# First dense product of the graph layer computed with its result already turned; weight scales from norms; late partial rows kept in SBUF

## What is computed

```
def gcn_conv(x, W, b, src, dst, n_nodes):
    h = x @ W
    deg = segment_sum(ones, dst); dinv = rsqrt(deg)
    msgs = h[src] * (dinv[src] * dinv[dst])[:, None]
    return segment_sum(msgs, dst) + b

# x + gcn_conv(relu(gcn_conv(layernorm(x), W1, b1)), W2, b2), then
xn = l2norm(layernorm(x)); logits = xn @ (scale * l2norm(phi))   # 32 x 32 slots
d_w, c_w = softmax(logits, over slots of an expert), softmax(logits, over all)
slots = einsum('bld,bles->besd', xn, d_w)
eo = gelu(slots @ w1 + b1) @ w2 + b2
return x + einsum('bkd,blk->bld', eo, c_w)
```

## Time and profile before

| | us |
|---|---|
| median of 3 runs | 3336.66 |
| lowest and highest | 3330.42 and 3339.79 |
| the profiled execution, own time | 3334.27 |
| its span in the trace | 3332.5 |
| PE busy in it | 3109.9 (93%) |
| DVE busy | 1899.1 (57%) |
| POOL busy | 1894.5 (57%) |
| ACT busy | 1152.4 (35%) |
| TensorE clock granted, mean | 0.975 of full |

### The profile page before, as it was taken

How to read it: one execution, slowest core, us unless ns; L and a number is a source line. 1 busy time by engine, 2 the same in 40 slices (tenths; PEclk the granted TensorE clock), 3 DMA queues, 4 the chain that set the end, 5 groups by cost and what they waited for, 6 DMA issues and landing times. The chain is left out here.

```text
span 3332.5 us, 55557 instructions
## 1 busy us (share of the span) xinstructions
PE 3109.9 (93%) x18917; PEld 1984.9 (60%) x18917; DVE 1899.1 (57%) x3045; ACT 1152.4 (35%) x1379; POOL 1894.5 (57%) x1804
## 2 busy tenths in 40 slices
PE   3769999999999999889999999999999998689998
PEld 1336766667676767555666666666666653345665
DVE  7864444444444444357777777777777773101332
ACT  4832332232322222234444444444444441111000
POOL 3377777777777777377666666666666631100000
PEclk8979999999999999899999999999999999889999
DMA  8789999999999999499989888999998879999995
GB/s 308 273 322 352 322 332 323 328 330 323 334 324 331 321 334 323 160 338 353 310 310 315 305 308 305 309 312 308 310 310 311 304 251 348 320 325 267 269 274 166
DMA packets 341258, 1021.87 MB, mean 307 GB/s; under 512 B 146808, under 2 KB 150162, under 8 KB 332016
## 3 DMA queue, kind: packets, MB, share of 16 engines
q0 software_dynamic: 137376, 664.09, 57.3%
q1 hardware_dynamic: 189416, 314.66, 29.1%
q10 hardware_dynamic: 14200, 39.58, 3.7%
HBM read 876.65 MB, written 135.08 MB: 304 GB/s over the span
## 5 line engine op out<-in xcount | busy, mean ns | idle before, releaser
L1570 POOL DMA_INDIRECT xs<-table,idx x833 | 873.4, 1049 | 481.7 <-PE m_part L1747 281.8
L1051 POOL DMA_INDIRECT xs<-table,idx x833 | 927.4, 1113 | 301.1 <-issue 186.4
L1747 PE MATMUL m_part<-xs 128*128 128x512 f16 (+1 forms) x3332 | 587.8, 329 | 27.9 <-DMA xs<-table,idx 22.0
L1321 PE MATMUL a_part<-xs 128*128 128x512 f16 (+1 forms) x3332 | 583.6, 329 | 30.5 <-DMA xs<-table,idx 19.6
L1303 PE MATMUL a_ps_o<-Ws,xs 128*128 128x512 f16 (+1 forms) x3456 | 577.6, 326 | 0.0
L1747 PEld LDWEIGHTS m_part<-xs 128*128 128x128 f16 x3332 | 418.6, 142 | 167.0 <-issue 47.1
L1321 PEld LDWEIGHTS a_part<-xs 128*128 128x128 f16 x3332 | 414.5, 142 | 159.9 <-issue 41.7
L1303 PEld LDWEIGHTS a_ps_o<-Ws,xs 128*128 128x128 f16 x3456 | 338.1, 98 | 219.3
L1776 PE MATMUL m_ps_l<-xs,m_xT 128*128 128x512 f16 x1764 | 388.7, 379 | 1.4 <-issue 1.3
L1763 PE MATMUL m_ps_s<-dw_mem,xn_mem 128*128 128x512 f16 x1296 | 311.3, 380 | 2.8 <-DVE xs L1637 2.8
L1776 PEld LDWEIGHTS m_ps_l<-xs,m_xT 128*128 128x128 f16 x1764 | 172.3, 98 | 208.8 <-issue 3.1
(11 more groups left out here) (413 smaller groups left out, 3700.5 us busy)
## 6 DMA issues: line engine op xcount, KB each, us to landing
xs<-in_L_ffn_w_dram SPq DMA_DIRECT2D x64, 1152.0 KB, 10.4
xs<-table SPq DMA_DIRECT2D x98, 384.0 KB, 6.2
xs<-table,idx POOLq DMA_INDIRECT x1666, 5.6
cw_dram<-xs SPq DMA_DIRECT2D x49, 512.0 KB
table<-arena SPq DMA_DIRECT2D x49, 384.0 KB, 3.7
table<-xs SPq DMA_DIRECT2D x49, 384.0 KB
xs<-x_pad SPq DMA_DIRECT2D x49, 384.0 KB, 5.9
x_dram<-xs SPq DMA_DIRECT2D x49, 384.0 KB, 5.6
```

What stands on the lines that cost most here:

```text
L1051: pool.indirect_dma_start(out=ring[:, t, :], out_offset=None, in_=table, in_offset=bass.IndirectOffsetOnAxis(ap=idx[:, k:k + 1], axis=0)). ...
L1321: mm = nc.tensor.matmul(part[:, bass.ds(to + a, z - a)], pick[:, i % 2, :, t], ring[:, n % RING, half * D + a:half * D + z], start=False, ...
L1570: pool.indirect_dma_start(out=ring[:, t, :], out_offset=None, in_=table, in_offset=bass.IndirectOffsetOnAxis(ap=idx[:, n:n + 1], axis=0)). ...
L1747: mm = nc.tensor.matmul(part[:, bass.ds(off + at, e - f)], pick[:, i % 2, :, t], ring[:, n % RING, half * D + f:half * D + e], start=False ...
```

## The change

1. The first dense product is computed with its roles exchanged: pieces of W1 (128x128) are the stationary operand, the turned rows `vT` move, 128 columns at a time. The result comes out turned, [feature, node], in six units of 128 features with 18 matmuls each (`hidden`), 108 in all in place of 36, laid into free columns of `ps_o` and `ps_t` (`unit_place`). The second turn on PE (12 transposes), its two copies, the bias step and the 768-wide ReLU and split are gone. For each unit DVE reads it, adds the bias per partition and multiplies by a factor per node (`hidden_read`), ACT takes the ReLU as the high half (`hidden_high`), and DVE writes the low half (`hidden_low`): 12 DVE and 6 ACT instructions of 128 columns for each bin.
2. The factor per node now lies along the free axis. It is turned once (one transpose), written to a DRAM tensor `fac_dram`, and SP loads for each bin one row of it, 512 bytes, to all partitions (`fac`).
3. The second product follows its bin by two iterations instead of three; PE's tail has one bin less, and the store follows by three instead of four.
4. The scales of the weights come from the square sum (ACT, `accum_out`, with a ones matmul across partitions and a root) in place of the largest magnitude; the preparation of the weights is put in another order.
5. In `mixture`, the results of units 16 to 30 are kept in SBUF, in places where the expert weights of the last groups have been (`kept`), and DVE adds them from there. 15 of the 31 stores to `part_dram` and 15 of its loads are gone.

```diff
+        def unit_place(m, c):
+            if m == last:
+                both = part[:, 0:P], part[:, 512:512 + P], part[:, 1024:1024 + P], part[:, 1536:1536 + P]
+            else:
+                both = (ps_o[:, D:D + P], ps_o[:, D + P:D + 2 * P]) * 2
+            return (*both[0:2], ps_s[:, 512 - P:512], ps_s[:, 1024 - P:1024], *both[2:4])[c]
+
+        def units_whole(m, c):
+            return DC * m + c + 1 + (m < last and c in (0, 4))
...
+                    m = i - 1
+                    if 0 <= m < NBR:
+                        of_m = own_block(sp, tab, m)
+                        wait(sp, h_read, DC * (m - 1))
+                        sp.dma_start(fac[:, m % 2, :], fac_dram[bass.ds(of_m, 1), :].to_broadcast([P, P])).then_inc(fac_in[m % 2], 16)
...
-                    j = i - 4
+                    j = i - 3
...
+                def hidden_high(i, c):
+                    k = DC * i + c
+                    act.wait_ge(h_read, k + 1)
+                    wait(act, prod2, i)
+                    nc.scalar.activation(hT[:, 0, c * P:(c + 1) * P], t_h[:, c, :], ACT.Relu).then_inc(ht_hi, 1)
...
-                    link(v.tensor_copy(wm[:, :], ps_o[:, 512:514]))
-                    link(v.scalar_tensor_tensor(bm[:, :], wm[:, 0:1], float(D), bm[:, :], ALU.mult, ALU.add))
+                def first_scale():
+                    v.wait_ge(f1_sum, 1)
+                    v.tensor_copy(fsum[:, 0:1], ps_s[:, 0:1]).then_inc(f1_read, 1)
+                    v.wait_ge(normed1, 1)
+                    link(v.tensor_scalar(bm[:, :], wm[:, 0:1], float(D) ** 0.5, None, ALU.mult))
...
-                weight_maxima()
                 choose(1)
+                first_scale()
...
                 add_own_rows(0)
+                first_low()
                 column_sums()
+                second_scale()
...
+                def hidden_read(i, c):
+                    v.wait_ge(prod1, units_whole(i, c))
+                    if c == 0:
+                        v.wait_ge(fac_in[i % 2], 16 * (i // 2 + 1))
+                        wait(v, ht_lo, DC * i)
+                    v.scalar_tensor_tensor(t_h[:, c, :], unit_place(i, c), bcol[:, c:c + 1], fac[:, i % 2, :], ALU.add, ALU.mult).then_inc(h_read, 1)
+
+                def hidden_low(i, c):
+                    v.wait_ge(ht_hi, DC * i + c + 1)
+                    wait(v, prod2, i)
+                    v.scalar_tensor_tensor(hT[:, 1, c * P:(c + 1) * P], t_h[:, c, :], 0.0, hT[:, 0, c * P:(c + 1) * P],
+                                           ALU.max, ALU.subtract).then_inc(ht_lo, 1)
...
+                def hidden(m, first, end):
+                    for c in range(first, end):
+                        if c == 4 and m < last:
+                            pe.wait_ge(h_read, DC * m + 2)
+                        for d in range(DC):
+                            for half, Wp in ((0, W1s[0]), (0, W1s[1]), (1, W1s[0])):
+                                mm = nc.tensor.matmul(unit_place(m, c), Wp[:, d, c * P:(c + 1) * P], vT[:, half, d * P:(d + 1) * P],
+                                                      start=(d == 0 and half == 0 and Wp is W1s[0]), stop=(d == DC - 1 and half == 1))
+                        mm.then_inc(prod1, 1)
...
-                    if i >= 3:
-                        pe.wait_ge(ht_hi, i - 2)
-                        pe.wait_ge(ht_lo, i - 2)
-                        pe.wait_ge(biased, i - 1)
-                        if i == 3:
-                            pe.wait_ge(lo2, DC)
+                    if i >= 2:
+                        second_waits(i - 2)
                         product(hT, W2s).then_inc(prod2, 1)
...
-                    if i >= 2:
-                        pe.wait_ge(h_lo, i - 1)
-                        pe.wait_ge(vt_hi, i)
-                        pe.wait_ge(vt_lo, i)
-                        turn(h2).then_inc(h_turned, 1)
...
-                        product(vT, W1s).then_inc(prod1, 1)
-                    steps(10, CT)
+                        wait(pe, t_lo, i - 1)
+                        hidden(i - 1, 0, 2)
+                    steps(9, 10)
+                    if i >= 1:
+                        hidden(i - 1, 2, 4)
+                    steps(10, 11)
+                    if i >= 1:
+                        hidden(i - 1, 4, DC)
+                    steps(11, CT)
...
+                        if k >= KEPT:
+                            act.wait_ge(up, NG - 1)
+                            if k >= KEPT + G * DC * H // D:
+                                act.wait_ge(down, NG)
+                            nc.scalar.activation(kept[k], ps_o[:, k % 2, 0:D], ACT.Copy, scale=inv[:, 0:1]).then_inc(act_done, 1)
+                            continue
```

More of the change, by code:

```diff
@@ L1018, in _ @@
             def _(sp):
-                for i in range(NBR + 4):
+                for i in range(NBR + 3):
                     if i < NBR:
@@ L1090, in t_high @@
                         wait(act, stored[j % 2], 16 * (j // 2))
[L1091 to L1093 removed]
+                        nc.scalar.activation(stage[:, j % 2, 0:D], ps_o[:, 0:D], ACT.Copy, scale=out2[:, 0:1]).then_inc(t_hi, 1)
+                def hidden_high(i, c):
[3 more added lines that the diff above has]
+                    nc.scalar.activation(hT[:, 0, c * P:(c + 1) * P], t_h[:, c, :], ACT.Relu).then_inc(ht_hi, 1)
+                for i in range(NBR + 1):
                     if i < NBR:
@@ L1311, in turn, with turn_v, hidden_waits, second_waits @@
                     return mm
+                def turn_v(m):
+                    pe.wait_ge(v_lo, m + 1)
+                    wait(pe, vt_hi, m)
+                    wait(pe, vt_lo, m)
+                    if m == 0:
+                        pe.wait_ge(f1_read, 1)
+                    if m == NORM_AT - 1:
+                        pe.wait_ge(rooted, 1)
+                    turn(v2).then_inc(v_turned, 1)
+                def hidden_waits(m):
+                    pe.wait_ge(vt_hi, m + 1)
+                    pe.wait_ge(vt_lo, m + 1)
+                    wait(pe, h_read, DC * m)
+                def hidden(m, first, end):
+                    for c in range(first, end):
+                        if c == 4 and m < last:
[5 more added lines that the diff above has]
+                        mm.then_inc(prod1, 1)
+                def second_waits(m):
+                    pe.wait_ge(ht_hi, DC * (m + 1))
+                    pe.wait_ge(ht_lo, DC * (m + 1))
+                    wait(pe, t_lo, m)
+                    if m == 0:
+                        pe.wait_ge(lo2, DC)
                 for i in range(NBR):
@@ L1844, in mixture @@
         assert LOW_AT < EARLY
+        KEPT = next(k for k, g in up_at.items() if g == NG - 2)
+        KEPT_DOWN = next(k for k, g in down_at.items() if g == NG - 1)
         w1s = (w1_first, w1_second)
```

244 lines of the change are left out of this document (110 added, 134 removed).

## The result

| | before | after |
|---|---|---|
| median, us | 3335.87 (3330.42 to 3339.79, 4 runs) | 3303.10 (3298.73 to 3308.97, 4 runs) |
| profiled execution, us | 3334.27 | 3298.73 |
| its span, granted clock | 3332.5, 0.975 | 3297.0, 0.979 |

The ratio is 0.9903, with a 95% interval of 0.9887 to 0.992: 32.8 us less by the medians, 35.5 us less from one profiled execution to the other. The forecast was 3296 us, 41 us less. Two further comparisons of the same kernel gave 3304.4 (0.9905) and 3304.1 us (0.990). The profiled execution was the fastest of its four, 4.4 us under their median, where the forecast had allowed 2.4.

A forecast was written before the change was run, and what follows sets the result against it. PE was taken to bound the steady bins, with gathers and wipes pacing the start. Terms 25.3 + 4.8 + 5.9 + 5 = 41.0 us off 3334.27 give 3293.3, as median 3296 us; forecast 3286 to 3303 (0.64), 8 in 10 from 3284 to 3320.

The forecast's parts named there:

- The steady bins: First layer: a bin falls from 24.11 to 23.56 us on PE, 25.3 us over 46 iterations.
- the tail: End of the first layer on PE: 20.3 us instead of 26.2, a gain of 5.9 us, bounds 4 and 7.
- the start: First bins of the first layer: bin 3 starts near 253.5 us instead of 258.34, 4.8 us gained, ends 0 and 8.
- a to e: Steady bins: turned-row copies, unit 4's wait for DVE, DVE's load, the last low half and SP's factor load stay hidden.
- (f), POOL: Steady bins: gathers nearly fill 24.1 us, read as slack; low halves taken as zero cost, +0.3 us a bin as rival.
- The rival of the weight loads: Steady bins: weight loads don't hide in long runs; a bin 4.05 us longer at 0.098, whole 3507 us; chance 0.10.
- the last unit's chain: Tail of the first layer: the last unit's chain, which nothing hides, adds 1.4 us.
- The mixture: Mixture: fewer stores shorten PE's waits for expert weights, 5 us gained, ends 0 and 10.
- the two waits named: Mixture: PE's waits for expert weights of 5.91 and 4.36 us; fewer stores can take the second off.

The follow-up runs named there:

- runs of 36 and 108: Changed kernel with the 108 short matmuls of a bin in one run instead of three of 36 with 4 long ones between: 3299.95 us, ratio 0.9894.
- fourteen: All profiled executions whose mixture was compared: four without kept rows took 559.2 us there on average, ten with them 552.6.
- the late load: Changed kernel with the 3 MB load of phi, and the squares made from it, four bins later in the first layer: 3300.05 us, ratio 0.9901.
- the changed kernel's second profile: The changed kernel itself, unedited, run again as the measure on the same chip: 3304.42 us, ratio 0.9905.

## Why the prediction was right, and where it was off

The measured median, 3303.10 us, lies in the range of 8 in 10, at the very edge of the forecast's own bracket (3286 to 3303). Its largest term was right in its mechanism and somewhat too large, the tail was right, and the start failed. The 35.5 us between the two profiled executions flatter the forecast: by the medians it is 32.8, and 0.9 of the 35.5 lie in the second layer, which the change doesn't touch.

**The steady bins: mechanism right, size 25.3 forecast, 21.9 measured.** The bin was to be 23.56 us and is 23.62, and before it was 24.10 in nearly all bins, not the 24.11 of the one that was read. (Each kernel has one bin that is 1.7 us longer, with four matmuls for the sum of phi's squares in it.) The largest part is the mis-sized short matmul: 0.0554 us taken from runs of 12, 0.0558 in runs of 36 and 108, so 6.03 and not 5.98 us for the product, 2.3 us over 46 bins; the other 0.02 us a bin are as small as the reading of a row. All that had to stay hidden stayed hidden (a to e): the line of the short matmuls shows 1.5 us of waits in the whole layer, none for DVE. (f), POOL: no wait for tiles in a steady bin, the six low halves hold a gather for nothing that shows, and the stretched gathers shrank (1.13 us busy for one in the earlier trace rows, 1.03 after). That reading, slack taken up, was right, but the slack was only 0.55 us a bin more than what was used.

**The rival of the weight loads is refuted** by the runs of 36 and of 108, both at 55.8 ns. The rule of the Trainium skill (TensorE: Matmul & The Clock Gate, section Back-to-back issue gap) of about 81 ns for a pair of 128 columns differs from this; the measurement decides. By the same section an isolated gap is 128/2.4 + 2.5 = 55.8 ns, and that is what the stream of fresh loads ran at here.

**The start: 4.8 forecast, 0.4 measured, the step that failed.** The prediction took bin 2's last gather at 245.96 and 5 to 6 us of landing for the end of that bin. In the changed kernel the wait for the wipe, the two turns and the product were out of the way as forecast, and then the gathers stood in their place: the median gather issued between 230 and 260 us took 11.7 us to land (6.2 in the steady bins), since 3 MB of phi fill the DMA engines there. The trace of before has the same stretch, in its busy time by stretch:

```profile
240.00:260.00 20.00, 18.52 (x122) 12.82 (x121) 7.44 (x10) 3.40 (x4) 15.43 (x16) 0.98 1.02 404
```

The prediction read a stretch from 166 to 250 us instead, in which this is averaged away to 0.88. It also put bin 3's start down to the wipes and the turns alone, though PE waited for gathered rows in that bin before the change too:

```profile
244.56 0.87 PE L1321 MATMUL a_part<-xs 128*128 128x512 f16 x4 [0.91 <-DMA xs<-table,idx]
245.91 0.86 PE L1321 MATMUL a_part<-xs 128*128 128x512 f16 x4 [0.49 <-DMA xs<-table,idx]
```

The load is in both kernels and costs both some 4 us there. So the 4.8 us compared a bin 3 without it (253.5) with one that had it (258.34), and booked the load's price as the change's gain. A second part: the prediction had DVE reach bin 0's sums some 2 us earlier, but its preparation now lies on bin 0's gathers and ends that bin some 2.6 us later (27.4 against 30.0 us from the same gather). From bin 0's end to bin 3 the changed kernel needs 50.7 us with the load out of the way and the kernel before 52.9 to 53.7; with the load in place it is 52.8 to 54.9 us in four executions, for 56.7 and 58.5. So the change gives 2 to 4 us behind bin 0, and pays about as much in bin 0.

**The tail: 5.9 forecast, 5.8 measured**, with 20.4 for 20.3 us; the last unit's chain shows as 1.16 us.

**The mixture: 5 forecast, 6.3 in the pair of profiles, 6.6 over fourteen.** The later of the two waits named (4.36 us) went, with its burst at the lower clock (5.73 to 4.08 us). That the earlier one shrinks is not shown. (One figure of the prediction is off: 322 GB/s over 24.1 us are 7.8 MB, not 7.9; nothing hangs on it.)

**What was left out:** 0.9 us in the second layer, within its scatter (1364.2 to 1367.9 us over the profiles), which also swallowed the 3.4 us by which the late load's execution had started that layer earlier.

## What to carry to other kernels

A product whose result is wanted turned can be computed turned even if that makes three times as many matmuls with a fresh weight load each: at 128 moving columns and the full clock the loads cost next to nothing (6.03 us for 5.86), so compare columns and not instructions. Before a gain is booked for a wait that goes, look at the DMA share in exactly those 20 us and at the landing time of the transfers in them, and ask whether what fills them is in both kernels. A large one-off load is better cut into pieces that the spare bandwidth of a step can carry, for moved as a whole it took its price along here. Count a start from the first instruction of its stage: the first gather of the layer was issued anywhere from 169.5 to 174.3 us in these executions. And when PE is the bound, read how many tiles the producer is ahead: the lead, not the producer's busy share, tells how much of the next saving will count.

## What the runs showed of the hardware

- 108 matmuls of 128 moving columns, each with its own load of 128x128 weights (98 ns), follow each other at 55.8 ns at the full clock.
- GpSimd's busy share doesn't show that the gathers bind: 309 and 312 us of 400 where TensorE never waited for them, 311 of 400 where it did. The lead does, 11 tiles and 6.
- A gather's landing time rose from 6.2 us to 11.7 us (median) under a 3 MB load on another queue, at 400 GB/s and a share of 1.01; at 366 GB/s, with the load in pieces of 0.5 MB, the median was 7.3 us and PE did not wait.
- TensorE's granted clock fell to 0.57 for 4 us (244 to 248, the changed kernel's second profile) behind 6 us in which four waits for rows had left the engine busy for 3.1.
- A gather of 0.95 us lasted 4.02 us when VectorE ran its last 768-column low half and then an addition of 2.55 us with two SBUF inputs beside it, and 1.56 us when the addition was moved away.
